# One fused four-layer kernel: the two token halves of a feed-forward block issued as one run of tiles

## The reference, cut to what matters

```python
# L0_xattn: for each of 4 experts (hidden 256), y = (silu(x@Wg.T) * (x@Wu.T)) @ Wd, masked by token id; Wg=Wu=Wd=ctx
# L0_ffn:   w1q, w3q, w2q = ternary weights, hidden 682
g = jax.nn.silu(x @ w1q.T) * (x @ w3q.T);  y = g @ w2q.T
# L1_ffn (its shared expert): hidden 352, plus a router and 8 experts
sh = jax.nn.silu(x @ sh_gate_W.T) * (x @ sh_up_W.T) @ sh_down_W.T
# L2_ffn:   ternary weights, hidden 704
hidden = jax.nn.sigmoid(x @ w1t.T) * (x @ w2t.T);  y = hidden @ w3t.T
x = x + y          # after each of the steps
```

## Time and profile before

| | |
|---|---|
| median of 3 runs | 1076.54 us (1074.39 to 1076.83) |
| the profiled execution's own time | 1081.43 us |
| its span in the trace | 1079.7 us |
| TensorE products busy | 884.0 us (82%) |
| VectorE busy | 739.6 us (69%) |
| ScalarE busy | 458.2 us (42%) |

### The profile page before, as it was taken

One profiled execution on the slowest core, in us unless ns is written; L12 is line 12 of the kernel. 1 busy time (PEld: TensorE's weight loads), 2 busy tenths in 40 slices (PEclk: granted clock), 3 DMA queues, 4 the chain that ended last, 5 costly groups with the idle time before them and its releaser, 6 DMA issues.

```text
span 1079.7 us, 11762 instructions
## 1 busy us (share of the span) xinstructions
PE 884.0 (82%) x4286; PEld 525.0 (49%) x4286; DVE 739.6 (69%) x974; ACT 458.2 (42%) x695; POOL 141.3 (13%) x222
## 2 busy tenths in 40 slices
PE   5999794489799999998997676777777898878796
PEld 3434562245655555544554333444345566644554
DVE  1775558954567887786687988888843436659773
ACT  2213436642333322121223888988933435422110
POOL 1000000000024334425000111111110000001111
PEclk8899886589989999998999555555577879889898
DMA  9500003100222220420009699787830000000000
GB/s 267 170 0 1 1 0 46 20 3 6 31 32 43 44 39 4 79 37 0 1 10 173 120 162 170 128 136 130 139 50 17 1 0 1 1 1 0 10 10 19
DMA packets 202204, 56.78 MB, mean 53 GB/s; under 512 B 182990, under 2 KB 200484, under 8 KB 202148
## 3 DMA queue, kind: packets, MB, share of 16 engines
q1 hardware_dynamic: 202036, 55.87, 27.7%
q10 hardware_dynamic: 112, 0.17, 0.1%
HBM read 20.62 MB, written 1.05 MB: 20 GB/s over the span
## 4 chain that ended last, share of the span: by engine, by line
PE 52%; DVE 25%; ACT 9%; issue 6%; DMA 6%; ACTq 1%; POOL 1%; POOLq 0%; DVEq 0%; SPq 0%
PE ps L874 48%; DMA arena<-xc 5%; ACT xc L1774 3%; DVE arena L2458 3%; PE ps L452 2%; ACT arena L1784 1%; DVE arena L2090 1%; DVE xn_t L1907 1%; PE ps L1004 1%; DVE sq L2369 1%; DVE sq L2366 1%; DVE arena L2467 1%; ACT arena_split L1691 1%; DVE xc L2262 1%; PE ps L1316 1%
## 5 line engine op out<-in xcount | busy, mean ns | idle before, releaser
L874 PE MATMUL ps<-arena 128*128 128x16 f16 (+7 forms) x1760 | 269.2, 324 | 68.1 <-ACT xc L1774 30.2
L874 PE MATMUL ps<-arena_split 128*128 128x512 f32 (+5 forms) x736 | 205.5, 443 | 25.5 <-DVE arena_split L1928 14.6
L874 PEld LDWEIGHTS ps<-arena 128*128 128x128 f16 (+4 forms) x1760 | 133.0, 130 | 178.7 <-issue 82.0
L874 PEld LDWEIGHTS ps<-arena_split 128*128 128x128 f32 (+5 forms) x736 | 138.0, 201 | 98.0 <-issue 38.1
L2458 DVE TENSOR_REDUCE arena<-ps 128x1 f32<-128x1024 f32 x128 | 152.4, 1221 | 27.8 <-PE ps L874 25.9
L1774 ACT ACTIVATE xc<-ps,arena 128x1024 int16<-128x1024 f32 x128 | 153.2, 1202 | 24.9 <-POOL arena L850 21.1
L874 PE MATMUL ps<-sq,arena 128*64 128x256 f32 (+3 forms) x256 | 80.9, 515 | 8.0 <-DVE sq L2369 7.9
L1558 ACT ACTIVATE act_buf<-ps 128x512 f32<-128x512 f32 (+2 forms) x34 | 20.3, 596 | 98.5 <-PE ps L874 98.5
L850 POOL TENSOR_SCALAR arena<-arena 128x1 f32<-128x1 f32 x128 | 34.0, 265 | 212.9 <-DVE arena L2458 212.9
L822 POOL TENSOR_SCALAR arena<-arena 128x512 f32<-128x512 f32 x12 | 23.1, 1923 | 248.0 <-DVE arena L2284 248.0
L452 PE MATMUL ps<-ident,arena 128*128 128x128 f32 (+4 forms) x194 | 34.5, 324 | 20.7 <-DMA arena<-in_x 6.6
(11 more groups left out here) (279 smaller groups left out, 1299.8 us busy)
## 6 DMA issues: line engine op xcount, KB each, us to landing
arena<-in_L_ffn_w SPq DMA_DIRECT2D x4, 640.0 KB, 6.1
arena_split<-arena_split SPq DMA_DIRECT2D x59, 32.0 KB
arena<-xc SPq DMA_TRANSPOSE x96, 3.3
arena<-in_x SPq DMA_DIRECT2D x1, 1024.0 KB, 5.6
arena<-in_ctx SPq DMA_DIRECT2D x1, 1024.0 KB, 8.1
arena<-in_L_xattn_Wkv SPq DMA_DIRECT2D x2, 512.0 KB, 4.0
arena<-in_L_ffn_gate_w SPq DMA_DIRECT2D x1, 1024.0 KB, 10.0
arena<-in_L_ffn_up_w SPq DMA_DIRECT2D x1, 1024.0 KB, 12.5
```

Source lines behind the costliest of these rows:

```text
L874: return pe.matmul(o, l, r, start=start, stop=stop)
```

## The change

`ffn` no longer ends a half before it begins the next. On TensorE `down` lags by `lag` tiles across the border of the halves, so that the second half's first one or two gate and up products stand ahead of the first half's last `down` products. ScalarE's and VectorE's `hidden_high` and `hidden_low` follow in the same way, and VectorE's `add_y` of the first half comes after the gate of the second half's tile `lag - 1`. For blocks of six tiles `ln_steps` now depends on the half: the first half's norm starts a tile earlier and its `xn` two, the second half's a tile later up to `rows`.

```diff
+        def ffn_lag(s):
+
+            return 2 if s["split"] else 1
...
-        def ln_steps(n):
+        def ln_steps(n, h):
             if n < 6:
                 return dict(mean=0, xc=0, sq=1, var=1, sd=2, diag=2, rows=2, xn=2, parts=2)
+            if n == 6 and h == 0:
+                return dict(mean=0, xc=0, sq=1, var=1, sd=2, diag=2, rows=3, xn=3, parts=4)
             if n == 6:
-                return dict(mean=1, xc=1, sq=2, var=2, sd=3, diag=3, rows=4, xn=5, parts=5)
+                return dict(mean=2, xc=2, sq=3, var=3, sd=4, diag=4, rows=5, xn=5, parts=5)
             return dict(mean=1, xc=1, sq=2, var=3, sd=4, diag=4, rows=5, xn=6, parts=7)
...
                         last.then_inc(hid_ready, 1)
-                        if i >= lag:
-                            down(i - lag)
+
+                        if h * s["n"] + i >= lag:
+                            down(*divmod(h * s["n"] + i - lag, s["n"]))
...
-                    for i in range(s["n"] - lag, s["n"]):
-                        down(i)
+                for i in range(s["n"] - lag, s["n"]):
+                    down(TH - 1, i)
...
-                        if s["split"] and i:
-                            hidden_high(s, h, i - 1)
+                        if s["split"] and h * s["n"] + i:
+                            hidden_high(s, *divmod(h * s["n"] + i - 1, s["n"]))
...
-                    if s["split"]:
-                        hidden_high(s, h, s["n"] - 1)
+                if s["split"]:
+                    hidden_high(s, TH - 1, s["n"] - 1)
...
+                def summed(h):
+                    dve.wait_ge(hid_used, s["u0"] + (h + 1) * s["n"])
+                    add_y(h, y_scale).then_inc(x_ready, 1)
...
-                        if s["split"] and i:
-                            hidden_low(s, h, i - 1)
+                        if s["split"] and h * s["n"] + i:
+                            hidden_low(s, *divmod(h * s["n"] + i - 1, s["n"]))
+                        if h and i == ffn_lag(s) - 1:
+                            summed(h - 1)
                         if between:
                             between(h * s["n"] + i)
...
-                    if s["split"]:
-                        hidden_low(s, h, s["n"] - 1)
-                    dve.wait_ge(hid_used, s["u0"] + (h + 1) * s["n"])
-                    add_y(h, y_scale).then_inc(x_ready, 1)
+                if s["split"]:
+                    hidden_low(s, TH - 1, s["n"] - 1)
+                summed(TH - 1)
```

More of the change, by code:

```diff
@@ L912, in ffn, with down @@
                 L = LN[s["name"]]
-                at = ln_steps(s["n"])
                 name = s["name"]
-                lag = 2 if s["split"] else 1
+                lag = ffn_lag(s)
+                def down(h, i):
+                    u = s["u0"] + h * s["n"] + i
+                    if s["split"]:
+                        v = s["v0"] + h * s["n"] + i
+                        pe.wait_ge(hid_low, v + 1)
+                        hid = [hid_parts[name][:, v % 3, j, :] for j in range(2)]
+                    else:
+                        pe.wait_ge(gated, u + 1)
+                        hid = [hid_buf[:, u % 2, :]]
+                    if i == 0:
+                        pe.wait_ge(x_ready, 2 * L + h + 2)
+                    r = s["rows"][i]
+                    for o in range(KC):
+                        for part in hid:
+                            last = mm(ps[:, 4 + o, :], s["w2"](i, o), part[0:r], i == 0 and part is hid[0],
+                                      i == s["n"] - 1 and part is hid[-1])
+                    last.then_inc(hid_used, 1)
                 for h in range(TH):
+                    at = ln_steps(s["n"], h)
                     if s["split"]:
@@ L923, in ffn @@
                     norm = INSIDE[name][h]
-                    def down(i):
-                        u = s["u0"] + h * s["n"] + i
-                        if s["split"]:
[L928 to L942, removed]
                     for i in range(s["n"]):
```

## The result

The changed kernel takes 1066.8 us (median of 5 runs, 1066.05 to 1068.52), the kernel before 1076.8 us (median of 5, 1074.39 to 1080.08). The ratio is 0.9899 [0.9879, 0.9919]: 10 us, 1.0%, faster. Timed again, as `e5_after_again`, the changed kernel gave 0.9899 [0.9873, 0.9924]. The forecast was 1068.6 us.

What follows compares the result with a forecast made beforehand. No engine was taken as the limit everywhere; TensorE's waits at the half borders and the slow clock behind them cost time. Waits -4.8 and clock -3.1 gave -7.9 us, from 1076.54 to 1068.6 us, range 1063.0 to 1074.0.

Steps and rivals of the forecast that it cites:

- waits on remainders at the border: TensorE's waits for `hidden_low` before the first half's last two `down` in `l0` and `l2` all go: -8.8 us.
- longer wait for `sq`, `l0` and `l2`: TensorE's wait before the first half's `var` grows by 1.1 us in `l0` and 1.0 us in `l2`.
- first `down` waits for `add_y`: The second half's first `down` waits for the first half's `add_y`: +0.7 us in each of `l0` and `l2`.
- first products wait for `xn_low`: The second half's first products wait for the split tokens: +0.5 us in `l0`, none in `l2`.
- clock: slow products at the border: Half-clock products behind the border's long wait go, 3.6 us in `l0` and 2.5 us in `l2`: -6.1 us.
- clock: longer fall at the first norm: Behind the first half's `var` the clock's fall lasts twice as long, 1.5 us more a block: +3.0 us.
- clock: second norm: No added cost at the second half's norm; as a bound, another 1.5 us fall there in `l0`.
- The zeros: In the blocks `l0x` and `l1` the change gains nothing, within 0.5 and 0.7 us to either side.
- The signs named: Expected in `l0` and `l2`: no border remainder waits, `sq` wait 2.2 to 2.6 us, `add_y` wait below 1, clock 1.00.
- The first, that the clock stays up at the norms: Rival: no clock fall at the norms of `l0` and `l2` either; -15.4 us, 1061.1 us, chance 0.10.
- The second, that short waits keep the clock low: Rival: border waits go but products stay slow; -1.8 us, 1074.7 us, no measurable change, chance 0.14.
- The third, the slower one: Rival: half clock from the first `var` through the first half's rest; +3.4 us, 1079.9 us, chance 0.06.

Runs made afterwards that it cites:

- e5_after_again: The changed kernel itself, unaltered, timed and profiled again: 1066.6 us (6 runs), 0.9899 of the kernel before.
- e2_steps_only: The changed kernel's new norm steps, but each half ended before the next begins in all four blocks: 1073.2 us, 0.9965 of the kernel before.
- e3_border_unsplit_only: The kernel before, with the halves run together only in `l0x` and `l1` and the old norm steps: 1079.8 us, 1.0016 of the kernel before.
- e1_old_steps: The changed kernel's order of products across the border, but with the old norm steps: 1085.4 us, 1.0072 of the kernel before.
- e4_var_later: The changed kernel with the variance products of both norms of a six-tile block one tile later: 1050.2 us, 0.9747 of the kernel before.
- e8_var_later_no_border: The changed kernel with `var` one tile later, but each half ended before the next begins in all blocks: 1051.8 us, 0.9760 of the kernel before.

## Why the prediction was right, point by point

The mechanism, its two places and the sign held. The sum was -7.9 us, -10.0 was measured by the medians, and by the profiles the two blocks are 9.1 us shorter. The idle time is where the forecast is confirmed; the clock term came out near, and this is in part luck, since the mean of -2.4 us is smaller than the 3.8 us between two profiles of one kernel. The forecast gave its range twice, once as -12 to -3.5 us (1064.5 to 1073.0) and once as 1063.0 to 1074.0; the measured time lies inside both. Term by term, the rows above against it:

| term | forecast, us | measured, us |
|---|---|---|
| waits on remainders at the border | -8.8 | -8.8, none left |
| longer wait for `sq`, `l0` and `l2` | +1.1, +1.0 | +0.93, +0.91 |
| first `down` waits for `add_y` | +0.7, +0.7 | +0.26, 0 |
| first products wait for `xn_low` | +0.5, 0 | +0.66, 0 (second profile 0.32) |
| all idle time of the two blocks | -4.8 | -6.7 |
| clock: slow products at the border | -6.1 | -5.1 |
| clock: longer fall at the first norm | +3.0 | +2.4 |
| clock: second norm | 0 | +0.5 |
| clock, all of the two blocks | -3.1 | -2.4 |

The rows on the clock are means of two profiles each. The border is the time of the 20 products behind the long wait, over 4.72 us: 8.31 and 7.06 us in `l0`, 7.18 and 6.44 in `l2`. The norms are the time from `var` to `rows`.

**The waits.** The wait for `sq` came to 2.24 and 2.15 us, where 2.4 was laid from the rows of ScalarE. The mis-sized term is the one for `add_y`. I had set a handover of 3.5 us against 2.8 us of products; the wait was 0.26 us in `l0`, and in `l2` none. The handover was right: in `l0` the activation of tile 7 begins at 135.55 and `add_y` ends at 138.81, 3.26 us later. The products were too cheap: TensorE's row ends at 138.70, and another row of 12 of them at full clock takes 3.36 us (141.28), where I had 12 x 0.236 = 2.8. The 0.236 us are right from start to start inside a row of gate and up products, and too little for a mixed row. Counting with that, the listed waits give -8.8 + 1.8 + 0.3 + 0.5 (mean of 0.66 and 0.32) = -6.2. The rest of the 6.7 is in the second half: the second last `down` of `l2` waits 0.43 us in one profile where about 1.06 stood, and in the second 1.16, and a wait of 0.16 us before `rows` in `l0` is gone. I had costed the second half's later steps at nothing, which was near enough. Of the 8.8 us of waits, 5.3 go by the earlier norm steps alone (`e2_steps_only`). I had laid most of it to the products that fill the wait and named the moved split in passing; the larger part is the split's.

**The clock.** At the border it is 1.00 in both blocks, as said. The time from the start of the first `var` to the start of `rows` tells the fall behind it; at full clock it is 7.6 to 7.8 us. In `l2` it is 8.98 us before (833.11 to 842.09) and 10.59 after (825.15 to 835.74), 1.6 more: the term of +1.5. In the second profiles it is 7.61 before (836.56 to 844.17), no fall at all, and 10.58 after. In `l0` it is 9.02 before (116.31 to 125.33) and 10.89 after; but in the second profiles 10.60 (115.17 to 125.77) before and 9.01 (112.64 to 121.65) after, the other way round. So "the fall lasts twice as long" holds in three of four profiled places of the changed kernel and is no fixed price. The bound I named, another fall at the second `var` of `l0`, came true in both profiles (8.04 us for 24 products above; 7.38 in the second). The second profile of the kernel before has it too, at 7.39. What the earlier trace rows showed as a place that "had escaped" was one execution's luck.

**The zeros.** `l0x` and `l1`: nothing, by `e3_border_unsplit_only`. In `l0x` the wait for `add_y` grew to 1.34 us, and `l0` still started no later. `l1` lasts from its first product to the router's `ident` 32.71 us before (226.94 to 259.65) and 32.02 after (222.10 to 254.12), and 0.5 of this 0.7 us is the block's first row of products, 4.13 us before and 3.60 after.

**The signs named.** No wait on a remainder stands at the border, the wait for `sq` is 2.24 and 2.15 us where 2.2 to 2.6 was named, the one for `add_y` below 1 us, and the border's clock at 1.00. The two blocks were to be 3 to 5 us shorter each; by the means they are 5.0 (`l0`) and 4.1 us (`l2`).

**The rivals.** The first, that the clock stays up at the norms, did not come about: half clock stands at 116 to 119. For this kernel the rule of the Trainium skill ("TensorE: Matmul & The Clock Gate", "Loop structure matters more than you think"), by which a long wait for data costs the clock, names no wait as short as the 1.2 to 2.2 us that went with falls here. The second, that short waits keep the clock low, is refuted at the border: waits of 0.66 and 0.26 us there went with a clock of 1.00. The same page's warning of many short idles ("A second HAM failure mode: psum-queue depth-cycling") did not apply to them. The third, the slower one, needed half clock for 39 products; the rows show at most the 24 behind `var`, and not all of them. What turned the sign in `e1_old_steps` was another thing, that I had taken in as a part of the change and not as a condition: without the earlier norm steps the kernel is 0.7% slower than before.

**What the forecast didn't see** is that the wait it let grow was the larger prize. Of the 15.4 us between the two blocks' mean in the changed kernel (112.6 us) and their time in `e4_var_later`, 8.0 are idle time and 7.3 busy time, by these stretches of its profile:

```profile
105.74:157.66 51.92, 46.42 (x188) 32.76 (x188) 35.05 (x50) 22.98 (x33) 0.00 (x0) 0.93 0.00 1
808.24:853.55 45.31, 44.30 (x184) 32.05 (x184) 24.25 (x34) 22.07 (x34) 0.00 (x0) 0.95 0.00 1
```

**What stays open.** What the merged border is worth once `var` is late: `e4_var_later` and `e8_var_later_no_border` can't be told apart by their times. Their profiles give it 2.7 us less idle time in the two blocks (6.51 us against 9.20), and 2.2 us more busy time at the same products, which is the term that differs by chance. And why the clock sometimes falls where TensorE waits only 0.30 us ahead: it did behind the first `var` of `l0` in `e4_var_later`, and did not there in `e8_var_later_no_border`, so the place alone doesn't decide it. What does, no run here shows.

## What to carry to other kernels

When an engine's program is made to run ahead over a border, lay out the whole chain that its first work beyond the border waits for, and move that chain first: here the same reordering cost 8 us, saved 6, or made no difference that the times can tell, by where the norm stood. A step that waits for a chain over other engines belongs one unit of independent work later than the chain takes; two numbers of that kind were worth 16.6 us (1066.8 to 1050.2), more than the whole reordering. Judge the idle time from one profile, but a term of the clock from several, since it alone differs by microseconds between executions of the same code.

## What the runs showed of the hardware beyond the forecast

- One-column products need not lower the clock: behind no wait of their own, 16 of them take 1.84 us and the 12 products after them 2.94 to 3.03 us, full speed, in seven of the eight places of `e4_var_later` and `e8_var_later_no_border`. In the eighth it is 4.59 us. Behind a wait of 1.2 to 2.2 us on the same engine 24 products take 7.3 to 8.6 us instead of 5.8 in 13 of the 16 places of the four profiles of the kernel before and the changed one, and 5.7 to 5.8 us in the other three.
- Filling the wait with two more products, whose results nobody uses, shortened the program by 5.3 us by the medians (0.9842 [0.9815, 0.9869] against 0.9899 [0.9873, 0.9924]).
- What the clock takes behind the same wait differs between executions: 9.02 and 10.60 us from `var` to `rows` in `l0` of the kernel before, 10.89 and 9.01 in the changed one.
